# One core, decoder of two layers: the weights' stage with its loads issued by two engines and waited for in groups

## The reference, cut to what matters

```
x = _layernorm(x + _L0_attn_ref(x, w_q, w_k, w_v, w_o))            # causal, ternary weights (BitLinear)
x = _layernorm(x + _L0_xattn_ref(x, ctx, mask, wq, bq, ... wo, bo)) # cross attention with RoPE
x = _layernorm(x + _L0_ffn_ref(x, W1, b1, ... Wg, bg))             # 8 experts, 2 per token
x = _layernorm(x + _L1_attn_ref(x, W_q, Wd_kv, W_uv, W_uk, W_o, gamma, beta))
x = _layernorm(x + _L1_xattn_ref(x, ctx, ctx))
x = _layernorm(x + _L1_ffn_ref(x, W_q, keys, down_embed, ...))     # retrieval over 512 embeddings, and an MLP

# inside _bitlinear, for each of the four weights of the first block:
sw = 1.0 / clip(mean(abs(w)), 1e-5);  wq = clip(round(w * sw), -1, 1) / sw
# of L1_attn only this is done once for all tokens:
absorbed_k = (W_q @ W_uk).reshape(H, DH, L)
```

## Time and the profile before

| | |
|---|---|
| median of three runs | 1569.18 us |
| the three runs | 1567.50 to 1570.98 us |
| the profiled execution's own time | 1567.79 us |
| its span | 1566.0 us |
| mean granted TensorE clock | 0.92 |

### The profile page before, as it was taken

One profiled execution on the slowest core, in us unless ns is written; L12 is line 12 of the kernel. 1 busy time (PEld: TensorE's weight loads), 2 busy tenths in 40 slices (PEclk: granted clock), 3 DMA queues, 4 the chain that ended last, 5 costly groups with the idle time before them and its releaser, 6 DMA issues. The chain is left out here.

```text
span 1566.0 us, 29490 instructions
## 1 busy us (share of the span) xinstructions
PE 1329.8 (85%) x9235; PEld 878.3 (56%) x9235; DVE 989.1 (63%) x3393; ACT 627.4 (40%) x1413; POOL 442.5 (28%) x612
## 2 busy tenths in 40 slices
PE   2468999999999945899999983788899986899997
PEld 1245566665665522566666642556666643688886
DVE  5368888888888533222222223588888862678886
ACT  0223555555555521222222222356666643343331
POOL 3234243342442001011111003566666330101100
PEclk9568999999999976999999995699999997799999
DMA  3234344443443134711111104765555420300000
GB/s 94 54 65 77 59 88 64 77 77 63 82 69 44 21 115 156 242 34 35 34 31 34 31 31 87 157 129 129 124 125 126 105 63 18 81 1 14 15 1 27
DMA packets 165944, 112.75 MB, mean 72 GB/s; under 512 B 32786, under 2 KB 155922, under 8 KB 165664
## 3 DMA queue, kind: packets, MB, share of 16 engines
q1 hardware_dynamic: 150880, 99.04, 28.1%
q0 software_dynamic: 3408, 9.31, 2.5%
q10 hardware_dynamic: 11504, 2.53, 0.9%
HBM read 46.48 MB, written 12.45 MB: 38 GB/s over the span
## 5 line engine op out<-in xcount | busy, mean ns | idle before, releaser
L894 ACT ACTIVATE first_probs<-pair 128x512 f32<-128x512 f32 x320 | 189.1, 597 | 160.5 <-PE pair L409 155.8
L1058 DVE CUSTOM_DVE_ANT_0 first_masked<-bank,kept_mask_q 128x256 bf16<-128x256 f32 x512 | 189.7, 418 | 16.3 <-PE bank L394 15.9
L394 PE MATMUL bank<-kept_stack_cross 96*128 96x256 bf16 x768 | 152.4, 282 | 15.7 <-DVE first_negmax_x L1058 9.6
L409 PE MATMUL pair<-kept_stack_cross 98*128 98x256 bf16 x768 | 148.4, 275 | 1.8 <-ACT second_probs L1924 1.6
L1446 PE MATMUL pair<-kept_w,experts_hidden_t 128*128 x312 | 141.6, 597 | 0.0
L1924 ACT ACTIVATE second_probs<-pair 128x512 f32<-128x512 f32 x192 | 112.0, 597 | 68.8 <-PE pair L409 66.9
L1487 ACT ACTIVATE experts_hidden_t<-bank,kept_b 128x128 f32<-128x128 f32 x156 | 44.6, 369 | 190.0 <-PE bank L1421 190.0
L1401 POOL DMA_INDIRECT experts_expert_rows<-x_mid,kept_row_of x39 | 37.1, 950 | 279.5 <-PE bank L1413 252.9
L394 PEld LDWEIGHTS bank<-kept_stack_cross 96*128 96x128 bf16 x768 | 65.8, 101 | 66.5 <-issue 24.6
L1446 PEld LDWEIGHTS pair<-kept_w,experts_hidden_t 128*128 128x128 f32 x312 | 60.0, 193 | 75.8 <-issue 75.8
L402 PE MATMUL pair<-kept_mask_t,kept_ident 128*128 128x512 bf16 x256 | 98.2, 383 | 1.2 <-ACT first_probs L894 1.2
(11 more groups left out here) (448 smaller groups left out, 3013.7 us busy)
## 6 DMA issues: line engine op xcount, KB each, us to landing
kept_stack_self<-first_parts_a SPq DMA_DIRECT2D x128, 64.0 KB, 3.2
kept_w<-in_L_ffn_W SPq DMA_DIRECT2D x16, 512.0 KB, 7.6
kept_w<-in_L_ffn_W SPq DMA_DIRECT2D x8, 1024.0 KB, 7.3
kept_stack_self<-second_parts_a SPq DMA_DIRECT2D x128, 64.0 KB, 3.6
kept_stack_cross<-first_parts_x_k SPq DMA_DIRECT2D x96, 64.0 KB
kept_stack_cross<-first_parts_x_q SPq DMA_DIRECT2D x96, 64.0 KB
kept_stack_cross<-second_parts_x_k SPq DMA_DIRECT2D x96, 64.0 KB
kept_stack_cross<-second_parts_x_q SPq DMA_DIRECT2D x96, 64.0 KB
```

Of the source, the lines that this page charges most:

```text
L394: mm = pe.matmul(out, q, k, start=mask is None, stop=True, skip_group_check=True)
L409: mm = pe.matmul(out, k, q, start=mask is None, stop=True, skip_group_check=True)
L894: act.activation(probs[i % RING][:, :], key_bank[i % 2][:, :], ACT.Exp, scale=att.scale).then_inc(probs_made, 1)
L1058: ins = dve.tensor_tensor_reduce(masked[(2 * i + a) % 16][:, :], score_bank[i % 2][:, a * D:(a + 1) * D], t["mask_q"][:, a, :], -1.0, 3.0e ...
```

## The change

All of it is in `prepare_weights`. The single list and single wait become groups with semaphores of their own: `raw_loads` (one semaphore for each of the four BitLinear weights), the identity, `cast_loads` (two masks and `before`), `permuted_loads` (6), `turned_loads` (6) and `used_loads` (15, used by later stages only). SP issues every second load of the raw, permuted and turned groups, then the eight bias loads and the sixteen rows of ones. ScalarE issues the other halves, the identity, the three cast loads, and later the fifteen `used_loads` and the two of `keys`. Between these it clears the third `stack_cross0` buffer with four activations of 96 x 1024 from a tile of zeros, which VectorE now clears first, and makes three casts that were VectorE's. GpSimd clears the first buffer as before and the second only after `tern_made`. VectorE's cast of the identity moves behind the four sums, and the sums wait for one weight each. VectorE waits for the permuted group where it waited for all of `loads`, and TensorE waits for the turned group ahead of the blocks that read it.

The core of the diff:

```diff
+        zeros = sb("zeros", [P, 1024])
...
+        cast_loads = [(causal_q[:, :], d["c_causal_q"]), (causal_t[:, :], d["c_causal_t"]), (t["before"][:, :], d["c_before"])]
...
         @block.sync
         def _(sp):
-            for dst, src in first_loads:
-                sp.dma_start(dst, src, allow_slow_non_contiguous=True).then_inc(first_loaded, 16)
-            for dst, src in loads:
-                sp.dma_start(dst, src, allow_slow_non_contiguous=True).then_inc(loaded, 16)
+            for dst, src, raw in raw_loads[0::2]:
+                sp.dma_start(dst, src, allow_slow_non_contiguous=True).then_inc(raw, 16)
+            for dst, src in permuted_loads[0::2]:
+                sp.dma_start(dst, src, allow_slow_non_contiguous=True).then_inc(permuted_loaded, 16)
+            for dst, src in turned_loads[0::2]:
+                sp.dma_start(dst, src, allow_slow_non_contiguous=True).then_inc(turned_loaded, 16)
             sp.wait_ge(bv_cleared, 1)
             for dst, src in bv_loads:
                 sp.dma_start(dst, src, allow_slow_non_contiguous=True).then_inc(bv_loaded, 16)
             sp.wait_ge(constants_made, 4)
-            sp.wait_ge(keys_cleared, 1)
+            for to in ones_rows:
+                sp.dma_start(to, ones_row[0:2, :, :]).then_inc(rows_set, 16)
+            sp.wait_ge(rows_set, 16 * len(ones_rows))
+
+        @block.scalar
+        def _(act):
+            for dst, src, raw in raw_loads[1::2]:
+                act.dma_start(dst, src, allow_slow_non_contiguous=True).then_inc(raw, 16)
+            act.dma_start(t["ident"][:, :], d["c_ident"]).then_inc(ident_loaded, 16)
+            for dst, src in cast_loads:
+                act.dma_start(dst, src, allow_slow_non_contiguous=True).then_inc(cast_loaded, 16)
+            for dst, src in permuted_loads[1::2]:
+                act.dma_start(dst, src, allow_slow_non_contiguous=True).then_inc(permuted_loaded, 16)
+            for dst, src in turned_loads[1::2]:
+                act.dma_start(dst, src, allow_slow_non_contiguous=True).then_inc(turned_loaded, 16)
+            act.wait_ge(zeros_made, 1)
+            last = t["stack_cross0"][2][0:CROSS0.rows, :, :, :].bitcast(F32).rearrange("r s g c -> r (s g c)")
+            for n in range(4):
+                act.activation(last[:, n * 1024:(n + 1) * 1024], zeros[0:CROSS0.rows, :], ACT.Copy).then_inc(casts_made, 1)
+            act.wait_ge(cast_loaded, 16 * len(cast_loads))
+            act.activation(t["causal_q"][:, :], causal_q[:, :], ACT.Copy).then_inc(casts_made, 1)
+            act.activation(t["causal_t"][:, :], causal_t[:, :], ACT.Copy).then_inc(casts_made, 1)
+            act.activation(t["before16"][:, :], t["before"][:, :], ACT.Copy).then_inc(casts_made, 1)
+            act.wait_ge(small_cleared, 1)
+            for dst, src in used_loads:
+                act.dma_start(dst, src, allow_slow_non_contiguous=True).then_inc(used_loaded, 16)
+            act.wait_ge(keys_cleared, 1)
             for h in range(2):
-                sp.dma_start(t["keys"][h * NKEY:(h + 1) * NKEY, h * NKEY:(h + 1) * NKEY], d["L1_ffn_keys"][h]).then_inc(keys_loaded, 16)
-            moved = 0
-            for att in (SELF0, CROSS0):
-                for stack in t[f"stack_{att.name}"]:
-                    for g in range(0, att.groups, 4):
-
-                        rows = stack[att.rows:att.rows + 2]
-                        sp.dma_start(rows[:, g:g + 4, D:2 * D] if att.causal else rows[:, 1, g:g + 4, :],
-                                     ones_row[0:2, :, :]).then_inc(rows_set, 16)
-                        moved += 16
-            sp.wait_ge(keys_loaded, 32)
-            sp.wait_ge(rows_set, moved)
+                act.dma_start(t["keys"][h * NKEY:(h + 1) * NKEY, h * NKEY:(h + 1) * NKEY], d["L1_ffn_keys"][h]).then_inc(keys_loaded, 16)
+            act.wait_ge(used_loaded, 16 * len(used_loads))
+            act.wait_ge(keys_loaded, 32)
+            act.wait_ge(casts_made, 7)
...
             pool.memset(ones_row[:, :, :], 1.0).then_inc(constants_made, 1)
-            for stack in t["stack_cross0"]:
-                pool.memset(stack[0:CROSS0.rows, :, :, :].bitcast(F32), 0.0)
+            pool.memset(t["stack_cross0"][0][0:CROSS0.rows, :, :, :].bitcast(F32), 0.0)
+            pool.wait_ge(tern_made, 1)
+            pool.memset(t["stack_cross0"][1][0:CROSS0.rows, :, :, :].bitcast(F32), 0.0)
...
+            dve.memset(zeros[:, :], 0.0).then_inc(zeros_made, 1)
...
-            dve.wait_ge(first_loaded, 16 * len(first_loads))
-            dve.tensor_copy(t["ident16"][:, :], t["ident"][:, :])
-
             for w in range(4):
+                dve.wait_ge(raw_loaded[w], 16 * KT)
                 dve.tensor_reduce(abs4[:, w:w + 1], raw4[:, w, :, :], AX.XY, ALU.add, apply_absolute_value=True)\
                     .then_inc(abs_summed, 1)
+            dve.wait_ge(ident_loaded, 16)
+            dve.tensor_copy(t["ident16"][:, :], t["ident"][:, :])
...
-            dve.wait_ge(loaded, 16 * len(loads))
-
+            dve.wait_ge(permuted_loaded, 16 * len(permuted_loads))
...
-            dve.tensor_copy(t["causal_q"][:, :], causal_q[:, :])
-            dve.tensor_copy(t["causal_t"][:, :], causal_t[:, :])
-            dve.tensor_copy(t["before16"][:, :], t["before"][:, :])
...
+            dve.wait_ge(turned_loaded, 16 * len(turned_loads))
...
+                if n == n_own:
+                    pe.wait_ge(turned_loaded, 16 * len(turned_loads))
```

More of the change, by code:

```diff
@@ L134, in prepare_weights @@
         ones_row = sb("ones_row_bf", [P, 2, 512], BF16)
-        first_loaded, loaded, rest_made = sem("first_weights_loaded"), sem("weights_loaded"), sem("rest_made")
+        raw_loaded, ident_loaded, rest_made = [sem(f"attention_weights_loaded_{n}") for n in range(4)], sem("identity_loaded"), sem("rest_made")
+        cast_loaded, permuted_loaded, turned_loaded, used_loaded = (
+            sem(f"{n}_loaded") for n in ("cast", "permuted", "turned_weights", "used_later"))
+        casts_made, zeros_made = sem("casts_made"), sem("zeros_made")
         constants_made = sem("constants_made")
@@ L139, in prepare_weights @@
         turned, copied = sem("turned"), sem("copied")
-        keys_cleared, keys_loaded = sem("keys_cleared"), sem("keys_loaded")
+        keys_cleared, keys_loaded, small_cleared = sem("keys_cleared"), sem("keys_loaded"), sem("small_cleared")
         absorbed_made, absorbed_copied = sem("absorbed_made"), sem("absorbed_copied")
@@ L143, in prepare_weights @@
         bv_cleared, bv_loaded, bv_turned = sem("bv_cleared"), sem("bv_loaded"), sem("bv_turned")
[L145 to L149, removed]
+        raw_loads = []
         for n, w in enumerate(("L0_attn_w_q", "L0_attn_w_k", "L0_attn_w_v", "L0_attn_w_o")):
@@ L168, in prepare_weights @@
             (t["beta"][0:LAT, :], d["L1_attn_beta"].rearrange("(p o) -> p o", o=1)),
+            (t["sum_of1"][:, :], d["c_sum_of"]), (t["by_row"][:, :, :], d["c_by_row"]),
+            (t["wq_ret"][:, :, :], d["L1_ffn_W_q"].rearrange("(t p) n -> p t n", p=P)),
         ]
@@ L171, in prepare_weights @@
         bv_loads = [(bv_wide[16 * n:16 * n + XC, :], bv_by_group[n // 2, n % 2]) for n in range(SHARED)]
[L172 to L181, removed]
+        ones_rows = []
+        for att in (SELF0, CROSS0):
+            for stack in t[f"stack_{att.name}"]:
+                for g in range(0, att.groups, 4):
+                    rows = stack[att.rows:att.rows + 2]
+                    ones_rows.append(rows[:, g:g + 4, D:2 * D] if att.causal else rows[:, 1, g:g + 4, :])
         bank = [ps[n][:, 0:P] for n in range(4)]
@@ L194, in prepare_weights @@
         turns += [(wd_perm[:, j, :], t["wd_t"][:, j, :]) for j in range(KT)]
+        n_own = len(turns)
         turns += [(wq1_raw[:, j, e * P:(e + 1) * P], wq1_t[:, e, j * P:(j + 1) * P]) for j in range(KT) for e in range(KT)]
@@ L241, in _ @@
             dve.memset(t["gamma"][LAT:P, :], 0.0)
-            dve.memset(t["beta"][LAT:P, :], 0.0)
+            dve.memset(t["beta"][LAT:P, :], 0.0).then_inc(small_cleared, 1)
             dve.memset(t["absorbed_t"][LAT:P, :, :], 0.0)
```

22 lines of the change are left out of this document (16 added, 6 removed).

## The result

The changed kernel takes 1552.11 us (median of six runs, 1549.36 to 1555.40), the kernel before, run beside it, 1568.34 us (six runs, 1565.00 to 1570.98). The ratio is 0.9897, with a 95% interval from 0.9875 to 0.9918: about 16 us less. The forecast was 1558.2, with 1553.5 as the low end of its range. Only the first of the two leaves out the forecast's 11.0 us.

The account below looks back on a forecast made before the run. SP's serial issuing was taken to bound the weights' stage; with ScalarE ending last at 27.6 us, the next stage starts at 28.8 instead of 39.82, 11.0 us gained, so 1569.18 becomes 1558.2 us, range 1553.5 to 1562.5.

Parts of the forecast that it names:

- What bounds the stage: Weights' stage: SP's serial issuing, about 0.585 us a load, sets the end at 38.8 us; bytes are not the limit.
- The rival that a second issuer brings nothing: Weights' stage: the transfers themselves are the limit, so the time stays at 1569.2 us; chance 0.02.
- SP's sum: Weights' stage: SP's ten loads, eight biases, sixteen rows of ones and the landing end at 20.4 us.
- VectorE's sum: Weights' stage: VectorE's chain, shorter by 3.5, 3.64 and 0.81 us, ends at 26.4, or 26.8 with GpSimd's hold.
- GpSimd's late clear: Weights' stage: the second clear, 14.7 to 18.2 us, holds VectorE's copies; taken at 0.4 us, bounds 0 and 3.5.
- the rival of 3.5 us: Weights' stage: the late clear holds all of VectorE's copies, VectorE ends at 29.9, total 1560.3 us; chance 0.13.
- ScalarE's sum: Weights' stage: issues, table load, clear, casts, fifteen `used_loads` and keys in a line end last, at 27.6 us.
- The rivals with a slow ScalarE: Weights' stage: ScalarE later by 2 to 6 us, 1560 to 1564, chance 0.12; or 1.249 us an issue, 1578.6, chance 0.03.
- The stages behind: From the first load of x on: every stage as long as before, only starting earlier by the 11.0 us gained.
- a rival on the clock: Next stage's first matmuls: clock comes down later, they run at full speed, 1 to 4 us more gained; chance 0.07.

Follow-up runs that it names:

- one_issuer: The changed kernel with every load and copy issued by SP again, waits, casts and clears kept as changed; ratio 0.9993 of the kernel before.
- split_only: The kernel before with only the issuing split, ScalarE issuing every second load of the two lists; ratio 0.9959 of the kernel before.
- early_clears: The changed kernel with GpSimd's second clear right behind its first, without waiting for the ternary weights; ratio 0.9921 of the kernel before.
- pool_clears: The changed kernel with all three large clears on GpSimd in a row, none on ScalarE, no tile of zeros; a single run, 1555.70 us.
- after_route_late: The changed kernel with thirteen small copies issued by SP and waited for at the end of the first attentions; ratio 0.9987 of the kernel before.
- before_later: The kernel before with the sixteen rows of ones laid three times, first load of x at 62.6 us; a single run, 1586.87 us.
- after: The changed kernel as first measured and profiled, against the kernel before: 1552.11 us, ratio 0.9897.
- after_again: The changed kernel unaltered, measured and profiled a second time: 1557.06 us against 1567.51 for the kernel before, ratio 0.9918.
- before_late: The kernel before with the sixteen rows of ones laid a second time, first load of x at 51.5 us; ratio 1.0085 of the kernel before.
- after_held: The changed kernel with SP issuing nineteen more copies of rows of ones before the stage's barrier; ratio 0.9969 of the kernel before.

## Why the prediction was right and wrong

**What bounds the stage: right.** SP's count of issues set the end. With it restored in one_issuer the whole gain is gone (0.9993), though VectorE ended at 27.74. The rival that a second issuer brings nothing is refuted by split_only. The Trainium skill's page "DMA: Bandwidth & Descriptors", section "Issuing engines are not separate DMA queues", has the mechanism right, since only the time of issuing is saved; its "usually small" does not fit this stage, where that was the bound and the split alone saved 6.9 us.

**SP's sum: 2.2 us short, no effect.** 20.4 forecast; its last row of ones was issued by 21.06 and it was through at 22.6. The rows of ones took 0.68 us each (8.18/12) beside ScalarE's issuing, against 0.61 before.

**VectorE's sum: right within 0.7 us.** Forecast 26.8, measured 27.52. The sums, at 6.9 to 8.7 and 0.68 us long, were through at 9.4 (forecast 9.1), the totals read at 10.14 (9.9), the ternary weights made at 14.91 (14.7), the sixteen copies through at 17.73 (17.5). The last 0.3 us came at L364, where TensorE's products took 1.42 us instead of 1.08, with the granted clock at 1.00 from 25 to 28 us here as from 32 to 34 before. This differs from execution to execution: over the thirteen profiles VectorE waited 0.64 to 1.53 us for these products, 0.64 and 1.09 in the two of the kernel before. No run shows why.

**GpSimd's late clear: right at the low end.** Taken at 0.4 us, measured at 0.5 by early_clears. Copies out of the banks were not held (2.44 us for sixteen, twice), so the rival of 3.5 us is refuted. The Trainium skill's "SBUF — State Buffer", section "Who interferes with whom", had it: the copies within SBUF are held, by a whole instruction, and a tensor_reduce never is. pool_clears shows both in a few lines, and that the hold can last beyond the instruction that is running: its cast outlasted the end of one clear at 9.05 us and ended with the next, at 12.56.

**ScalarE's sum: wrong by 3 us, in a step that did not decide.** The prediction set activations and issues in a line: 27.6. Measured, its last issue began at 22.5 and, at 2.0 us to landing as in the earlier trace rows, landed at about 24.5. The first fourteen issues were dearer than said (0.73 to 10.27, 0.68 each, not 0.585), and so were the fifteen later ones (12.02 to 21.94, 0.66 each). But the step that put the fifteen loads behind 6.3 us of activations failed: from 12.02 they ran beside them. The rivals with a slow ScalarE are refuted. The forecast of 28.8 for the next stage's first issue, against 28.42, came out well because the longer of two chains was taken, and VectorE's was only 0.8 us shorter in the forecast.

**The stages behind: the step that failed.** The prediction put it as "From the first load of x on, every stage as long as before", and so gave nothing to them. The measured 1552.11 lies 6.1 us below the 1558.2 forecast: 0.8 because the kernel before, run beside it, took 1568.34 and not 1569.18; 0.4 because the stage gained 11.4 and not 11.0; and the other 4.8 in the stages behind. In the first profile the experts' stage alone was 6.0 us shorter, 330.4 instead of 336.4. It has two lengths, 4.1 us apart on average, by when TensorE's clock rises. That this is not the change's contents is seen from both sides: after_route_late has them and the long stage, before_later lacks them and has the short one. What decides is not told by these runs beyond this: it goes with the moment at which the stage begins, and 595.0 and 595.3 us fell on different sides. The prediction had a rival on the clock, at 0.07, with the right size (1 to 4 us) and sign, but in the wrong place: the next stage's first 20 us ran at 0.50 as before (30 to 50 us in the profile after), and the gain came 560 us further on.

**How much of it the medians show.** In the medians, the time follows the start of the first attentions, and the clock's 4.1 us can hardly be told. The kernels with early rises, with what the earlier start alone gives, what it gives with 4.1 us more, and what was measured (us less than before, 95% interval):

| kernel | start alone | with the 4.1 | measured |
|---|---|---|---|
| after | 11.4 | 15.5 | 16.2 (12.9 to 19.6) |
| after_again | 10.4 | 14.5 | 12.9 (8.5 to 17.2) |
| early_clears | 12.3 | 16.4 | 12.4 (8.9 to 15.7) |
| split_only | 6.9 | 11.0 | 6.4 (3.3 to 9.6) |

The first's interval leaves out the start alone, that of after_again holds both, and those of the last two leave out the 4.1 us more. Of the kernels with late rises, before_late (11.7 later, 13.3 more), one_issuer (0.1 later, 1.1 less) and after_route_late (3.6 earlier in all, 2.0 less) agree with the start alone within their intervals; after_held does not (1.7 earlier, 4.9 less, 1.9 at the least). So the clock's step is shown in the profiled executions, and that every execution of the changed kernel gains it is not shown. The first measurement's 16.2 us may be part luck.

**What stays open.** The second attentions took 391.5 to 399.3 us over thirteen profiles, longest (398.0 to 399.3) in three that began it before 923 us; early_clears, beginning it at 921.5, took 393.9. No run varied this stage alone. And after_held's ratio lies 3 us below what its start and its experts' stage would give; with runs of it from 1558.65 to 1571.17 this may be chance, but no run shows that it is. So of the 16.2 us first measured, 11.4 are the stage, shown by the experiments. For the other 4.8, the profile has 4.0 in one execution: 6.0 gained by the experts and 1.7 ahead of them, 3.3 lost by the second attentions and 0.4 by the retrieval. How much of them lasts over many runs stays open. The second measurement, 12.9 us, holds the forecast's 11.0 within its interval.

## What to carry to other kernels

This preparing stage of some sixty small transfers was bound by their issuing on one queue, not by their bytes. In one like it, count issues per queue, and give the second issuing engine half of them before doing anything to waits or casts, since these pay only once the queue is no longer last. A stage that is merely started earlier need not hand down exactly the time saved: where TensorE came out of the routing at 1.2 GHz, its clock rose some 8 us earlier or later in the stage, worth 4 us in the profiled executions. So a range for a shift should hold such a step for a pause behind it. And one profile is one execution: before its stage lengths are taken for the kernel's, they want comparing with the medians. Keep long GpSimd clears clear of the first VectorE cast within SBUF, or get them done before it.

## What the runs showed of the hardware that was not expected

ScalarE's queue went on issuing transfers while its activations ran: `cos` was issued at 12.02 us while the first 96x1024 copy ran from 11.59 to 12.65. A VectorE cast of 128x128 was shown with 4.34 us, through what was left of one GpSimd clear and all of the next in line, and a reading of 128x4 from a bank behind it was shown with 3.52 us, ending with it. With SP and ScalarE issuing at the same time, ScalarE's issues cost 0.66 to 0.68 us each and SP's rows of ones 0.68, where SP alone had needed 0.61; SP's first ten loads took 0.59 each even so, as alone (0.585). And the same experts' stage, in kernels that differ only in what lies ahead of it, had TensorE's clock rise 8 to 9 or 15 to 18 us after its beginning; which of the two went with when the stage began.
